# Totals over partitions moved from TensorE to GpSimd from the fifth batch on, in a gated attention and ternary feed-forward kernel

## The reference

```python
# cross attention, linear in the sequence, 8 heads of 64, context c in the place of k and v
q = einsum("bcn,oc->bon", layernorm(x), Wq);  k = einsum("bcn,oc->bon", c, Wk);  v = einsum(..., c, Wv)
q = softmax(q, over the 64 of a head) * 64**-0.5;  k = softmax(k, over n)
context = einsum("bhdn,bhen->bhde", k, v);  out = einsum("bhde,bhdn->bhen", context, q)
out = Wo out + bo;  out = out / norm(out, over channels) * g * sqrt(128)
x = x + tanh(g_xattn) * out
# feed-forward, weights rounded to -1, 0, 1 times their mean magnitude
y = layernorm(x);  inter = bitlinear(y, w_gate) * bitlinear(y, w_up)        # 1024 -> 2752
x = x + tanh(g_ffn) * bitlinear(inter, w_down)                              # 2752 -> 1024
```

## Time and profile before

| | |
|---|---|
| time, median of 3 runs | 1369.78 us (1366.87 to 1372.92) |
| the profiled execution | 1372.63 us, of which 1370.8 us are the span of the trace |
| PE busy | 1301.8 us, 95% of the span |
| DVE busy | 979.2 us, 71% |
| ACT busy | 627.6 us, 46% |
| POOL busy | 573.4 us, 42% |
| granted clock of PE, mean | 0.98 of full speed |

### The profile page before, as it was taken

The page is one execution under the profiler, slowest core; times in us unless marked ns, Lnnn a source line. Parts: engine busy times, 40 slices in busy tenths (PEclk is TensorE's granted clock), DMA queues, the critical chain, the costliest instruction groups (busy, mean ns, idle before and its releaser), DMA issues. The chain is left out here.

```text
span 1370.8 us, 30040 instructions
## 1 busy us (share of the span) xinstructions
PE 1301.8 (95%) x12312; PEld 951.5 (69%) x12312; DVE 979.2 (71%) x1343; ACT 627.6 (46%) x879; POOL 573.4 (42%) x357
## 2 busy tenths in 40 slices
PE   4887699999999999999899999999999999999999
PEld 2444387755688658985498747885598748985994
DVE  6977778867898887788488856888578876633330
ACT  4668886853444334353335433453435443421220
POOL 0149935845454464454333533335145331422120
PEclk8998799999999999999999999999999999999999
DMA  9939999877555798888978778786979678646521
GB/s 355 408 139 331 306 281 307 243 159 174 124 146 140 169 241 216 204 199 197 161 181 199 154 170 200 178 184 148 230 156 227 143 148 184 185 137 164 162 72 46
DMA packets 408328, 266.33 MB, mean 194 GB/s; under 512 B 329152, under 2 KB 345920, under 8 KB 408192
## 3 DMA queue, kind: packets, MB, share of 16 engines
q1 hardware_dynamic: 401280, 239.25, 70.0%
q10 hardware_dynamic: 6912, 25.17, 5.4%
HBM read 158.66 MB, written 26.00 MB: 135 GB/s over the span
## 5 line engine op out<-in xcount | busy, mean ns | idle before, releaser
L1137 PE MATMUL ps<-w_dn,inter_buf 128*128 128x512 fp8e4 x1376 | 304.5, 379 | 2.2 <-ACT inter_buf L1149 2.2
L1137 PEld LDWEIGHTS ps<-w_dn,inter_buf 128*128 128x128 f16 x1376 | 134.6, 99 | 158.3 <-ACT inter_buf L1149 2.4
L1053 PE MATMUL ps<-zT,w_gu 128*128 128x256 f16 x1664 | 190.4, 274 | 3.0 <-DVE zT L1391 3.0
L1053 PEld LDWEIGHTS ps<-zT,w_gu 128*128 128x128 fp8e4 x1664 | 163.4, 99 | 28.0 <-DVE zT L1391 3.2
L1830 POOL TENSOR_TENSOR qs<-qs,q_stat 128x1024 f32<-128x1024 f32 x64 | 129.5, 2025 | 119.4 <-DVE q_stat L1634 119.0
L1088 PE MATMUL ps<-w_gu 128*128 128x128 f16 x2880 | 173.5, 219 | 0.0
L1088 PEld LDWEIGHTS ps<-w_gu 128*128 128x128 fp8e4 x2880 | 165.2, 98 | 2.5
L1888 POOL TENSOR_TENSOR w_gu<-w_gu 128x512 f32<-128x512 f32 x60 | 84.4, 1409 | 174.2 <-DVE w_gu L1741 117.4
L1741 DVE SCALAR_TENSOR_TENSOR w_gu<-ps,w_gu 128x512 f32<-128x512 f32 x120 | 82.3, 687 | 73.3 <-PE ps L1088 72.7
L1088 PE MATMUL ps<-zT,w_gu 128*128 128x128 f16 x2176 | 132.6, 219 | 0.8 <-DVE w_gu L1741 0.8
L1088 PEld LDWEIGHTS ps<-zT,w_gu 128*128 128x128 fp8e4 x2176 | 125.2, 98 | 3.0 <-issue 0.9
(11 more groups left out here) (196 smaller groups left out, 2531.4 us busy)
## 6 DMA issues: line engine op xcount, KB each, us to landing
w_gu<-forms SPq DMA_DIRECT2D x158, 256.0 KB, 4.1
ct_raw<-forms SPq DMA_DIRECT2D x52, 256.0 KB, 4.3
w_dn<-in_down_w SPq DMA_DIRECT2D x19, 512.0 KB, 5.8
xb<-in_x ACTq DMA_DIRECT2D x16, 512.0 KB, 6.3
x_dram<-xb SPq DMA_DIRECT2D x16, 512.0 KB, 3.3
fin<-x_dram SPq DMA_DIRECT2D x32, 256.0 KB, 3.6
out<-fin SPq DMA_DIRECT2D x32, 256.0 KB, 3.0
inter_buf<-in_up_w SPq DMA_DIRECT2D x15, 512.0 KB, 9.9
```

What stands on the lines that cost most here:

```text
L1053: last = nc.tensor.matmul(ps[:, rest_bank(g, j), s * T:s * T + T], w_gu[:, w, k, :], zT[:, h, k, :], start=(k == 0 and h == 0), stop=(k == ...
L1137: mm = nc.tensor.matmul(ps[:, down_bank(g, k), :], inter_of(g, j, u % 2, b), w_dn[:, j, hf * 512:hf * 512 + 512], start=(u == 0), stop=(u ...
```

## The change

From the fifth batch on (`i >= BY_DMA`, with `BY_DMA = 4`) `csum` and `msum` are no longer steps of PE but of POOL: `partition_all_reduce` with addition over 128 partitions, from `cmx` into a new one-column tile `c_tot` in SBUF, and from `mmx` into `m_tot`. `cscale` and `mscale` read these tiles and no longer PSUM. That is 12 context totals and 12 product-matrix totals; the first four batches keep theirs on PE. In the table below the lists of `mabs` and `msum` begin with the third batch, the others with the first. The totals take their places on POOL from the same table, and the table has new numbers for most steps behind the opening.

```diff
-    "cabs": [3, 36, 182, 259, 490, 740, 1054, 1144, 1579, 1812, 2008, 2203, 2420, 2649, 2817, 3139],
-    "csum": [30, 61, 192, 324, 660, 1010, 1071, 1312, 1677, 1869, 2066, 2282, 2486, 2742, 2897, 3152],
-    "cscale": [31, 69, 203, 348, 686, 994, 1059, 1313, 1690, 1879, 2065, 2318, 2511, 2741, 2930, 3161],
-    "mabs": [611, 880, 1017, 1305, 1483, 1654, 1883, 2097, 2329, 2540, 2756, 2948, 3154, 3355],
-    "msum": [614, 876, 1034, 1295, 1514, 1701, 1908, 2124, 2338, 2536, 2757, 2969, 3158, 3356],
-    "mscale": [120, 122, 622, 886, 1029, 1307, 1488, 1700, 1902, 2127, 2336, 2541, 2768, 2985, 3164, 3363],
+    "cabs": [3, 36, 182, 259, 490, 740, 1052, 1135, 1573, 1807, 2003, 2202, 2422, 2697, 2819, 3090],
+    "csum": [30, 61, 192, 324, 660, 819, 1053, 1250, 1596, 1825, 2053, 2285, 2400, 2700, 2801, 3124],
+    "cscale": [31, 69, 203, 348, 686, 925, 1061, 1309, 1597, 1829, 2065, 2304, 2469, 2725, 2835, 3135],
+    "mabs": [611, 885, 1029, 1299, 1483, 1660, 1885, 2104, 2327, 2529, 2750, 2930, 3159, 3359],
+    "msum": [614, 887, 1025, 1348, 1511, 1663, 1862, 2100, 2359, 2541, 2763, 2942, 3158, 3337],
+    "mscale": [120, 122, 622, 890, 1037, 1305, 1500, 1681, 1893, 2128, 2334, 2542, 2760, 2964, 3166, 3362],
...
@@ -499,6 +499,7 @@
         kmx, kbias, ksm = sb("kmx", [P, PAIRS]), sb("kbias", [P, PAIRS]), sb("ksm", [P, PAIRS])
         cmx, c_unit, c_per, k_unit, c_cut = (sb("cmx", [P, 1]), sb("c_unit", [P, 2]), sb("c_per", [P, 2]), sb("k_unit", [P, 2]),
                                              sb("c_cut", [P, 2]))
+        c_tot, m_tot = sb("c_tot", [P, 1]), sb("m_tot", [P, 1])
         mmx, m_unit, m_per, y_unit = sb("mmx", [P, 1]), sb("m_unit", [P, 1]), sb("m_per", [P, 1]), sb("y_unit", [P, 2])
         lmx, l_unit, l_per, l_used = sb("lmx", [P, 3]), sb("l_unit", [P, 3]), sb("l_per", [P, 3]), sb("l_used", [P, 3])
         mv = sb("mv", [P, 4])
@@ -863,6 +864,8 @@
                 proj_free[PROJ][0] = (l_ranged, x + 1)
 
             def csum(i, _):
+                if i >= BY_DMA:
+                    return
                 pe.wait_ge(started, 2)
                 wait(pe, c_max, i + 1)
                 wait_banks(proj_free[PROJ])
@@ -1495,7 +1500,7 @@
                     wait(dve, cc_lo_s, min(i - 1, BY_PE))
                 wait(dve, k_exp, PAIRS * (i - 1))
                 wait(dve, m_ranged, 3 * (i - 1))
-                nc.vector.tensor_scalar(c_unit[:, col], ps[:, PROJ, 0:1], TINY, 1.0 / TOP, ALU.max,
+                nc.vector.tensor_scalar(c_unit[:, col], ps[:, PROJ, 0:1] if i < BY_DMA else c_tot[:, :], TINY, 1.0 / TOP, ALU.max,
                                         ALU.mult).then_inc(c_ranged, 1)
                 wait(dve, c_ranged, i + 1)
                 nc.vector.reciprocal(c_per[:, col], c_unit[:, col]).then_inc(c_scaled, 1)
@@ -1594,7 +1599,7 @@
                     return
                 wait(dve, m_sum, paired(i + 1))
                 wait(dve, m_hi_s, paired(i))
-                nc.vector.tensor_scalar(m_unit[:, :], ps[:, TR, 0:1], TINY, 1.0 / TOP, ALU.max,
+                nc.vector.tensor_scalar(m_unit[:, :], ps[:, TR, 0:1] if i < BY_DMA else m_tot[:, :], TINY, 1.0 / TOP, ALU.max,
                                         ALU.mult).then_inc(m_ranged, 1)
                 wait(dve, m_ranged, 3 * i + 1)
                 nc.vector.reciprocal(m_per[:, :], m_unit[:, :]).then_inc(m_ranged, 1)
@@ -1838,6 +1843,20 @@
                 nc.gpsimd.tensor_tensor(rsv[:, hf, :], ssv[:, hf, :], neg_half.broadcast_to([P, 4]),
                                         ALU.pow).then_inc(rs_ready, 1)
 
+            def csum(i, _):
+                if i < BY_DMA:
+                    return
+                wait(pool, c_max, i + 1)
+                wait(pool, c_ranged, i)
+                nc.gpsimd.partition_all_reduce(c_tot[:, :], cmx[:, :], P, bass.bass_isa.ReduceOp.add).then_inc(c_sum, 1)
+
+            def msum(i, _):
+                if i < BY_DMA:
+                    return
+                wait(pool, m_max, paired(i + 1))
+                wait(pool, m_ranged, 3 * i)
+                nc.gpsimd.partition_all_reduce(m_tot[:, :], mmx[:, :], P, bass.bass_isa.ReduceOp.add).then_inc(m_sum, 1)
+
             def x2a(i, hf):
                 wait(pool, y_scaled, 2 * i + hf + 1)
                 wait(pool, xr_in[i % 2], 16 * (i // 2 + 1))
@@ -1888,7 +1907,7 @@
                 nc.gpsimd.tensor_tensor(v[:, :, 0, :], v[:, :, 0, :], v[:, :, 1, :], ALU.mult).then_inc(pair_muled, 1)
 
             program({"consts": consts, "wquant": wquant, "rstd1": rstd1_, "rstd2": rstd2_,
-                     "qnorm": qnorm, "q32": q32_, "q_lo": q_lo_, "z": z, "z_sum": z_sum, "form": form, "pair_mul": pair_mul, "rs": rs, "x2a": x2a})
+                     "qnorm": qnorm, "q32": q32_, "q_lo": q_lo_, "z": z, "z_sum": z_sum, "form": form, "pair_mul": pair_mul, "csum": csum, "msum": msum, "rs": rs, "x2a": x2a})
 
 
 def kernel(**inputs):
```

More of the change, by code:

```diff
@@ new lines @@
+    "mabs": [611, 885, 1029, 1299, 1483, 1660, 1885, 2104, 2327, 2529, 2750, 2930, 3159, 3359],
+    "msum": [614, 887, 1025, 1348, 1511, 1663, 1862, 2100, 2359, 2541, 2763, 2942, 3158, 3337],
+    "mscale": [120, 122, 622, 890, 1037, 1305, 1500, 1681, 1893, 2128, 2334, 2542, 2760, 2964, 3166, 3362],
+    "m_hi": [626, 886, 1036, 1310, 1499, 1709, 1891, 2149, 2333, 2556, 2759, 2973, 3179, 3358],
+    "m_lo": [648, 905, 1045, 1313, 1513, 1716, 1895, 2146, 2336, 2555, 2767, 2976, 3170, 3371],
+    "ld_xq": [2, 147, 369, 591, 865, 1031, 1219, 1466, 1697, 1911, 2123, 2306, 2570, 2753, 2987],
[3 rows of a table added]
@@ new lines @@
+    "qsum": [89, 106, 155, 168, 245, 275, 337, 360, 445, 482, 543, 596, 625, 743, 829, 891, 953, 963, 985, 1056,
[3 rows of a table added]
+    "qnorm": [93, 112, 159, 173, 255, 284, 351, 367, 466, 500, 550, 605, 630, 750, 836, 878, 957, 958, 1005, 1100,
[4 rows of a table added]
+    "e_f": [107, 134, 197, 205, 292, 310, 385, 395],
+    "qf_hi": [469, 517, 562, 700, 771, 820, 862, 918, 940, 975, 1021, 1078, 1127, 1147, 1230, 1321, 1391, 1409,
+        1431, 1584, 1615, 1656, 1688, 1742, 1801, 1866, 1903, 1946, 2012, 2074, 2132, 2181, 2240, 2270, 2321, 2370,
+        2472, 2492, 2534, 2599, 2663, 2720, 2783, 2807, 2855, 2926, 2939, 3040, 3061, 3127, 3197, 3218, 3288, 3331,
+        3405, 3431],
@@ new lines @@
+    "qf_lo": [479, 520, 565, 708, 783, 841, 911, 933, 964, 983, 1013, 1092, 1133, 1165, 1252, 1355, 1400, 1432,
+        1477, 1561, 1592, 1657, 1717, 1766, 1824, 1874, 1916, 1959, 2040, 2105, 2137, 2189, 2225, 2264, 2335, 2361,
+        2479, 2514, 2564, 2600, 2667, 2712, 2774, 2802, 2894, 2925, 2956, 3030, 3060, 3117, 3189, 3217, 3289, 3355,
+        3387, 3420],
+    "turn_q": [484, 524, 662, 714, 787, 844, 919, 920, 973, 991, 1023, 1084, 1141, 1213, 1328, 1345, 1394, 1414,
+        1530, 1575, 1632, 1676, 1724, 1762, 1828, 1881, 1938, 1944, 2066, 2092, 2154, 2196, 2234, 2263, 2341, 2362,
+        2484, 2508, 2546, 2602, 2672, 2739, 2769, 2782, 2914, 2915, 2979, 3017, 3097, 3108, 3193, 3221, 3306, 3341,
+        3376, 3433],
@@ L210 @@
+    "outp": [181, 184, 187, 189, 241, 244, 248, 249, 334, 340, 346, 350, 405, 410, 412, 414, 651, 652, 656, 657,
[6 rows of a table added]
+    "yev": [191, 256, 362, 417, 663, 758, 901, 967, 1044, 1124, 1317, 1405, 1515, 1616, 1729, 1797, 1928, 1988,
[3 rows of a table added]
+    "ssg": [202, 265, 368, 429, 672, 764, 938, 976, 1070, 1128, 1344, 1407, 1542, 1622, 1738, 1805, 1929, 1981,
[4 rows of a table added]
+    "ld_xr": [19, 151, 364, 606, 1027, 1163, 1537, 1559, 1945, 2069, 2376, 2378, 2758, 2910, 3199, 3434],
[8 rows of a table added]
     "zt": [356, 471],
@@ L247 @@
-    "form": [291, 1106, 1107, 1119, 1157, 1170, 1174, 1200, 1275, 1281, 1282, 1308, 1330, 1332, 1333, 1334, 1415,
-        1416, 1484, 1485],
-    "load_form": [1536, 1537, 1545, 1546, 1548, 1564, 1571, 1572, 1573, 1597, 1606, 1607, 1608, 1609, 1630, 1635,
[11 rows of a table removed]
-    "product": [1550, 1560, 1562, 1563, 1568, 1583, 1584, 1595, 1596, 1604, 1605, 1623, 1624, 1656, 1664, 1671,
[11 rows of a table removed]
-    "evict": [1533, 1534, 1535, 1543, 1544, 1565, 1582, 1592, 1593, 1615, 1616, 1621, 1627, 1626, 1628, 1646, 1667,
[11 rows of a table removed]
-    "pair_mul": [1547, 1629, 1653, 1669, 1682, 1728, 1748, 1749, 1830, 1831, 2082, 2091, 2092, 2100, 2109, 2115,
[3 rows of a table removed]
@@ new lines @@
+    "form": [291, 1102, 1106, 1140, 1164, 1169, 1183, 1207, 1266, 1270, 1277, 1284, 1326, 1327, 1376, 1377, 1408,
+        1447, 1493, 1494],
+    "load_form": [1502, 1503, 1504, 1505, 1536, 1541, 1543, 1544, 1554, 1578, 1604, 1605, 1610, 1611, 1620, 1621,
[11 rows of a table added]
+    "product": [1550, 1551, 1552, 1553, 1562, 1563, 1564, 1582, 1586, 1623, 1627, 1637, 1638, 1639, 1649, 1668,
[11 rows of a table added]
+    "evict": [1535, 1539, 1555, 1556, 1557, 1572, 1587, 1594, 1595, 1618, 1619, 1634, 1635, 1636, 1644, 1665, 1666,
[11 rows of a table added]
```

(12 more changed lines are left out.)

185 lines of the change are left out of this document (76 added, 109 removed), and 196 rows, old and new, of the table WHEN.

## The result

The changed kernel takes 1548.65 us (median of four runs, 1544.34 to 1551.5), the kernel before 1371.35 us beside it. The ratio is 1.1278, interval 1.125 to 1.1306: 177 us slower. The forecast of 1500 us was 49 us low; its range of 1385 to 1700 us holds the time. The profiled execution took 1544.34 us, its span 1542.5 us. In the new kernel the lines are shifted: L856 is L857, L1088 is L1093, L839 is L840, L1149 is L1154, L1597 is L1602, L1498 is L1503, L1830 is L1835, L1838 is L1843, L1888 is L1907; POOL's totals are L1851 and L1858.

What follows compares the result with a forecast made beforehand. PE was taken as the bound, busy 934.5 of 945 us in the main stretch. On the profiled 1372.6 us, plus 132 us for blocks on POOL, less 4.8 us: 1499.8 us, said as 1500; range 1385 to 1700 us.

Steps and rivals of the forecast that it cites:

- The block: On POOL, each total: a code load, the sum and a load back, 6.3 + 1.3 + 6.3 = 13.9 us.
- The way to PE: Late POOL steps hold ACT, whose `evict` steps then come late for PE: 5.5 us lost on PE per block.
- one mean gap of 4.4 us: POOL's mean wait in the stretch, taken to hide that much of each block, leaving later steps 9.5 us late.
- one slack of 4.0 us: Half of the 8.1 us between one `pair_mul` on POOL and its use by ACT, taken off the 9.5 us.
- The second way, through DVE to `outp`: A late product-matrix total delays `mscale` on DVE, making `outp` on PE 4.3 us late; counted within the 5.5 us.
- 24 blocks by 5.5 us are 132 us: The sum's main term: time that PE loses to the blocks on POOL.
- The 4.8 us given back: On PE, 24 totals removed at 0.20 us from start to start, taken off the time.
- no load at all: faster: Rival: the sum on POOL runs like other steps, nothing is late, PE gains 4.8 us: 1355 to 1369 us; chance 0.08.
- no gain, no loss: Rival: no load on POOL, but a sum near 4.1 us eats the 4.8 us: 1365 to 1375 us; chance 0.05.
- Half hidden: Rival: the load ahead runs while POOL waits for the total's input: 1390 to 1430 us; chance 0.19.
- POOL the bound: Rival: loads of 14.4 us make blocks of 30.1 us, overfilling POOL: over 1640 us; chance 0.12.
- The reordering: The new order of steps, counted at nothing; at most it collects PE's 10.5 us of idle time.

Runs made afterwards that it cites:

- the five sums that paid once: The changed kernel with four further sums, into a tile nobody reads, directly ahead of each total on POOL: 1598.9 us, ratio 1.1638.
- the kernel with the same PE instructions and no change of kind: The changed kernel with each of the 24 sums on POOL replaced by a one-column multiplication by one: 1370.77 us, ratio 0.9989.
- The halves: The kernel before with only the 12 context totals, or only the 12 product-matrix totals, on POOL: 1454.79 us (ratio 1.0616) and 1457.17 us (1.0624).
- the sums that nobody reads: The kernel before, totals still on PE, with 24 sums of a constant tile added on POOL behind the same waits: 1509.52 us, ratio 1.1004.
- the two kernels with an ordinary step and nothing added around it: 24 totals on POOL as one-column multiplications by one: in the changed kernel's order 1370.77 us (0.9989), in the order before 1375.73 us (1.0021).
- the steps that fill the time: The changed kernel with multiplications for sums, and dummy power steps on POOL ahead of and behind each, as long as the idle times: 1539.48 us, ratio 1.1198.

## Why the prediction was right and where it fell short

**The block was right, what fills it is open.** A total on POOL is a block of about 14 us in which POOL does nothing visible, paid on both sides of the sum and not shared between totals. The forecast was 13.9 us, 6.3 + 1.3 + 6.3; measured are 6.3 + 0.5 + 7.5 = 14.3 us. That its price was taken from the landing of a 512 KB transfer is luck: the profile counts 408328 DMA packets before and after, so none of the transfers that it records goes with the idle time, and no run shows what POOL does in it. That it loads code, as the prediction has it, fits the five sums that paid once, but is not shown. The Trainium skill gives a price for the first call of code that was just loaded: about 6 us, with no instruction visible in the profile (GPSIMD Engine Reference, section Instruction dispatch). The 6.3 us ahead of a sum agree with it, the 7.5 us behind one are longer. The runs show that the way back pays as well, at every total.

**The way to PE was right.** The forecast counted 132 us of waiting on PE. Against the kernel with the same PE instructions and no change of kind it is 132.7 us. The nearness of the two flatters the working: one mean gap of 4.4 us and one slack of 4.0 us stood for 24 places. The halves, at some 7.1 us of total time each block, and the sums that nobody reads bear out its main claim, that POOL's queue carries the loss. The second way, through DVE to `outp`, was counted in the same place and not added; the runs put it at some 20 us in the old order. It didn't make matrix totals dearer than context totals. Three readings in the working were off and weigh nothing in the sum: POOL's longest gap in the stretch was 16.9 us (ahead of `x2a`) and not 16.2; of ACT's waits, the 23 are those for `pair_mul` and the 17 those for `qnorm`; and two totals have as few as 2 other steps between them, not 3.

**The step that fell short is the sum's missing term.** "24 blocks by 5.5 us are 132 us" let PE lose only while it waits. It lost 43.0 us more while it worked, since its clock fell in and after its waits: 4.76 us of idle time, then 12 matmuls at a granted clock of 0.50. The row was there to ask about: in the opening the clock was 0.87 and 0.93 where PE idled, and 1.00 where it was full. In the kernel after the holes go on nearly to the end, and from 280 to 1400 us the mean clock is 0.94. With this term the forecast is 1497 + 43 = 1540 us.

**The 4.8 us given back didn't come.** PE's busy time did fall by 2.9 to 3.4 us in the two kernels with an ordinary step and nothing added around it, but neither is faster than the kernel before beyond its interval. In the old order most of the saving turned into a wait for `evict` on DVE. So the rival "no load at all: faster" would have been wrong even if its condition had held; "no gain, no loss" was its outcome, within 1 us. In the two orders that were run, totals on POOL without their price reach the time of the kernel before and no better.

**The other rivals.** "Half hidden" named the right condition, a load issued ahead of the wait, and it is met: one sum began 0.13 us behind its input. But the condition doesn't decide. POOL comes to the total so late that the input is mostly there already; in 22 of 24 cases the idle time stayed, 6.3 us each, though in seven of them the input came only while it ran. "POOL the bound" failed on the price: with 138.6 + 171.8 us of idle time and 580.1 us of work, POOL still has time in sum.

**What was to be seen.** Idle stretches around the totals: seen. `mscale` waiting some 5 us for POOL: 33.6 us in nine cases, 3.7 us each, 5.4 at most. PE's slices at 9 tenths or less with waits of L1088 (now L1093) and `outp` in front: seen, and deeper, down to 7. ACT's waits beyond 117.1 us: 160.2 us. The reordering, counted at nothing, is worth nothing within 0.3%.

## What to carry to other kernels

Price a step that is moved to another engine by what that engine ran before and after it, and not by its own duration: here half a microsecond of summing cost 14 us of queue, and a kind of step that an engine doesn't otherwise run is best grouped, since five in a row paid once. An engine that is busy 42% of the time is not free in place; ask who stands behind the step in its queue. And when a delay reaches a full TensorE, count its waits and then the slower clock behind them, here a third of the waits again (43.0 beside 132.7 us).

## What was not expected of the hardware

- TensorE's granted clock was 0.50 for the 12 matmuls right behind 4.76 us of idle time; over the kernel the same 12264 instructions were busy 43.0 us longer, at a mean clock of 0.939 against 0.979.
- What POOL does ahead of a sum across partitions starts before the sum's semaphore wait is met: with POOL free for 10.54 us, the sum began 0.13 us behind its input.
- The way back to ordinary arithmetic is longer in the profile than the way there: 7.5 against 6.3 us on average, whichever ordinary step comes next.
- With the change already made, a sum over 128 partitions of one column takes 0.39 to 0.57 us on average, about what a multiplication of one column takes in the same places (0.38 to 0.68 us in the two kernels that had it without the steps that fill the time).
